# Raw token rows carried through the expert slots and scattered back, with the third normalisation moved from ScalarE to GpSimd

## The reference

```
x = x + cross_attention_16_heads(layernorm(x), ctx)     # each head sees 4 rows of ctx
x = x + moe(layernorm(x))                               # top 1 of 16 experts
x = x + causal_attention(layernorm(x), ctx, ctx)        # one head, 77 rows of ctx
x = x + dense_ffn(layernorm(x)) + peer_experts(layernorm(x))

moe(h): gate = softmax(h @ Wg); idx = argmax(gate)
        loc = number of earlier tokens that chose the same expert
        row idx*256 + loc of a table holds the token, if loc < 256 (else its output is 0)
        y = relu(row @ w1[idx]) @ w2[idx];  output = y * gate[idx]
```

## Time and profile before

| what | value |
|---|---|
| median of three runs | 505.94 us (505.74 to 507.4) |
| profiled execution, span from first to last instruction | 506.4 us |
| PE, DVE, ACT, POOL busy over the span | 83%, 72%, 68%, 66% |
| mean granted TensorE clock | 0.892 of full |
| stage A, until the first product with w1 | 0 to 121.86 us |
| stage B, until the last matmul | 121.86 to 184.4 us |
| gathers before the first transpose of stage C | 184.4 to 195.1 us |
| stage C, until the first product search of stage D on DVE | 195.1 to 254.6 us |
| stage D | 254.6 to 506.4 us |

### The profile page before, as it was taken

The page is one execution under the profiler, slowest core; times in us unless marked ns, Lnnn a source line. Parts: engine busy times, 40 slices in busy tenths (PEclk is TensorE's granted clock), DMA queues, the critical chain, the costliest instruction groups (busy, mean ns, idle before and its releaser), DMA issues.

```text
span 506.4 us, 9519 instructions
## 1 busy us (share of the span) xinstructions
PE 420.5 (83%) x2592; PEld 342.9 (68%) x2592; DVE 363.5 (72%) x1469; ACT 345.3 (68%) x652; POOL 334.1 (66%) x269
## 2 busy tenths in 40 slices
PE   4877887964999953986877999999999999999877
PEld 3766766733998852875645776767767767777667
DVE  3457885520222214789689999999999999999991
ACT  1462546241222222699779999999999999999995
POOL 5235877762000017564049999999999999999995
PEclk9795998575999995568598999999999999999998
DMA  6982000102567611111000000000000000000000
GB/s 202 344 225 83 27 21 22 43 26 67 143 198 214 191 38 53 36 53 32 1 12 10 14 20 10 21 21 21 21 10 16 16 21 21 21 13 19 10 12 21
DMA packets 42417, 29.70 MB, mean 59 GB/s; under 512 B 4155, under 2 KB 38555, under 8 KB 42395
## 3 DMA queue, kind: packets, MB, share of 16 engines
q1 hardware_dynamic: 38539, 22.85, 15.7%
q0 software_dynamic: 2624, 6.30, 3.6%
q10 hardware_dynamic: 1232, 0.31, 0.3%
HBM read 18.95 MB, written 8.39 MB: 54 GB/s over the span
## 4 chain that ended last, share of the span: by engine, by line
POOL 31%; issue 9%; DVE 5%; ACT 5%; PE 3%; POOLq 1%; ACTq 0%; DVEq 0%
POOL arena_sb L497 20%; POOL arena_sb L489 10%; DVE picked_sb L1486 4%; ACT arena_sb L745 1%; ACT xh_sb L531 1%; ACT arena_sb L737 1%; ACT sc_sb L667 1%; PE banks L1062 1%; PE banks L1070 0%; PE banks L1016 0%; PE banks L1105 0%; PE banks L1114 0%; PE banks L1164 0%; PE banks L1034 0%; DVE cbn_sb L1368 0%
## 5 line engine op out<-in xcount | busy, mean ns | idle before, releaser
L497 POOL TENSOR_TENSOR arena_sb<-arena_sb,picked_sb 128x1096 f32<-128x1096 f32 (+1 forms) x46 | 152.2, 3337 | 10.6 <-DVE picked_sb L1486 8.1
L1486 DVE SCALAR_TENSOR_TENSOR picked_sb<-arena_sb,best_sb,banks 128x548 f32<-128x548 f32 x128 | 90.3, 778 | 0.2 <-POOL arena_sb L489 0.2
L745 ACT ACTIVATE arena_sb<-arena_sb,bsum_sb 128x548 f32<-128x548 f32 x124 | 83.1, 743 | 7.5 <-DVE bsum_sb L1494 5.4
L461 POOL DMA_INDIRECT picked_sb<-made,made_row_sb x32 | 30.9, 966 | 79.2 <-DMA made<-arena_sb 70.3
L489 POOL TENSOR_TENSOR arena_sb<-near_sb,sim_y_sb 128x1024 f32<-128x1024 f32 (+1 forms) x32 | 74.2, 2344 | 2.4 <-DVE near_sb L1451 2.3
L1105 PEld LDWEIGHTS banks<-ident_sb,arena_sb 128*128 128x128 f32 x496 | 57.6, 153 | 24.3 <-issue 16.6
L737 ACT ACTIVATE arena_sb<-arena_sb 128x2192 f32<-128x2192 f32 x32 | 65.6, 2049 | 0.2
L1105 PE MATMUL banks<-ident_sb,arena_sb 128*128 128x128 f32 x496 | 61.5, 278 | 4.5 <-ACT h_sb L723 3.1
L1095 PE MATMUL banks<-w_down_t_sb,h_sb 128*128 128x128 f32 x256 | 36.5, 289 | 9.3 <-DVE x_all_sb L1505 9.0
L1070 PEld LDWEIGHTS banks<-xt_sb,w_up_t_sb 128*128 128x128 f32 x256 | 31.1, 191 | 18.1 <-ACT w_t_sb L527 16.7
L1114 PE MATMUL banks<-up_e_sb,w_t_sb 128*128 128x128 f32 x256 | 36.0, 286 | 5.5 <-DVE picked_sb L1486 4.4
(11 more groups left out here) (182 smaller groups left out, 895.0 us busy)
## 6 DMA issues: line engine op xcount, KB each, us to landing
w_sb<-w SPq DMA_DIRECT2D x32, 256.0 KB, 3.2
x_all_sb<-x SPq DMA_DIRECT2D x8, 256.0 KB, 3.2
slots<-arena_sb POOLq DMA_DIRECT2D x4, 512.0 KB, 8.9
arena_sb<-slots SPq DMA_DIRECT2D x16, 128.0 KB, 3.1
made<-arena_sb SPq DMA_DIRECT2D x16, 128.0 KB, 1.9
xt_sb<-x_t_sb SPq DMA_DIRECT2D x32, 64.0 KB, 1.8
out<-x_all_sb SPq DMA_DIRECT2D x32, 64.0 KB, 1.5
ctx_t_sb<-ctx_t SPq DMA_DIRECT2D x8, 154.0 KB, 3.8
```

The lines of the kernel that those rows point to most:

```text
L497: pool.tensor_tensor(pp[p][:, heads, :], pp[p][:, heads, :], picked[p][:, heads, :], ALU.mult).then_inc(weighed, 1)
L745: ins = act.activation(pp[p][:, h, :], pp[p][:, h, :], ACT.Silu, scale=bsum[p][:, h:h + 1])
L1486: ins = dve.scalar_tensor_tensor(out=picked[p][:, h, :], in0=vv[p][:, h, 0:WIDE], scalar=best[p][:, h, TOP - 1:TOP], in1=scores_of(p), op0 ...
```

## The change

The tile of x in SBUF gets four more columns per token: `rstd`, shift, gate and the token's number. These 132 columns go to the slots as they are, so x is scattered raw.

- Stage A: `slot_rows` (ACT) goes. `choice_exps(j)` and `gates(j)` move forward in their lists, because `scatters(j)` now waits for the gate. `rows` has one instruction fewer. SP stores the eight blocks of x to a DRAM table `tokens`, each when its attention is added.
- Stage B: ACT normalises the loaded rows first (`slots_centred`, two activations per expert); PE's transposes wait for that. `rows_out` becomes two instructions that multiply by the gate and add the raw row. The store to `made` goes. POOL copies the token numbers of the loaded rows and issues two indirect transfers per expert that scatter the finished rows into `tokens`. SP loads the next rows of a buffer only after `rows_out` of the old ones and the copy of their numbers.
- Stage C: `gathers` and `combine` go. SP waits for all scatters and loads x back in eight transfers. `biases3` and ACT's `last_tokens` go; POOL normalises with four instructions per group.

```
@@ gpsimd
+            step(pool.iota(token_row, [[P, NT], [0, 1]], 0, 1))
...
             def scatters(i, p):
-                pool.wait_ge(xh_ready, 2 * i + p + 1)
+                pool.wait_ge(gate_ready, i + 1)
...
+            for e in range(NE):
+                b, nth = e % NBUF, e // NBUF
+                if nth:
+                    pool.wait_ge(y_out[b % 2], 32 * (2 * nth - 1 + b // 2))
+                pool.wait_ge(xe_in[b], 32 + 16 * nth)
+                pool.tensor_copy(token_of[b][:, :], xe[b][:, :, AT_TOKEN].bitcast(U32)).then_inc(token_of_ready, 1)
+                pool.wait_ge(tokens_kept, 16 * NB)
+                pool.wait_ge(y_ready, 1 + e + 1)
+                hold(pool, token_of_ready, 1 + e + 1)
+                for n in two:
+                    pool.indirect_dma_start(out=tokens, out_offset=bass.IndirectOffsetOnAxis(
+                        ap=token_of[b][:, n:n + 1], axis=0), in_=ye[b % 2][:, n, :], in_offset=None).then_inc(y_out[b % 2], 16)
+
+            def last_tokens(g):
                 p = g % 2
                 pool.wait_ge(croot3_ready, g + 1)
                 if g >= 2:
+                    pool.wait_ge(xt3_mm, g - 1)
+                for t in range(BT):
+                    ins = pool.tensor_scalar(xh[p][:, t, :], x_all[:, g * BT + t, 0:D], cmv3[p][:, t, 0:1], crstd[p][:, t:t + 1],
+                                             ALU.subtract, ALU.mult)
+                ins.then_inc(cxh_ready, 1)
@@ scalar, stage B
+                def slots_centred(b):
+                    act.wait_ge(xe_in[b], 32 + 16 * i)
+                    act.wait_ge(xet_mm, 1 + NBUF * i + max(b - 1, 0))
+                    for n in two:
+                        ins = act.activation(xe_n[b % 2][:, n, :], xe[b][:, n, 0:D], ACT.Identity,
+                                             bias=xe[b][:, n, AT_SHIFT:AT_SHIFT + 1], scale=xe[b][:, n, AT_RSTD:AT_RSTD + 1])
+                    ins.then_inc(xen_ready, 1)
+                slots_centred(0)
+                slots_centred(1)
                 slots_out(0)
                 slots_out(1)
                 for b in range(NBUF):
+                    if b + 2 < NBUF:
+                        slots_centred(b + 2)
                     relu_lo(b)
@@ sync
+            for half in range(NB):
+                sp.wait_ge(x1_ready, half + 1)
+                sp.dma_start(token_rows(half), x_all[:, half * BT:half * BT + BT, 0:D]).then_inc(tokens_kept, 16)
...
+                    sp.wait_ge(token_of_ready, 1 + NBUF * i + b + 1)
+                    sp.wait_ge(y_ready, 1 + NBUF * i + b + 1)
+                    load_slots(i + 1, b)
+                    load_expert(sp, i * NBUF + NBUF + b, b)
+            for p in two:
+                sp.wait_ge(y_out[p], 32 * (NE // 2))
+            for g in range(NB):
+                sp.dma_start(x_all[:, g * BT:g * BT + BT, 0:D], token_rows(g)).then_inc(x2_in[g], 16)
@@ vector
+            def rows_out(e):
+                b = e % NBUF
+                dve.wait_ge(y_mm, 1 + e + 1)
+                if e >= 2:
+                    dve.wait_ge(y_out[e % 2], 32 * (e // 2))
+                for n in two:
+                    ins = dve.scalar_tensor_tensor(out=ye[e % 2][:, n, :], in0=bank[6 + e % 2][:, n * D:(n + 1) * D],
+                                                   scalar=xe[b][:, n, AT_GATE:AT_GATE + 1], in1=xe[b][:, n, 0:D],
+                                                   op0=ALU.mult, op1=ALU.add)
+                ins.then_inc(y_ready, 1)
```

More of the change, by code:

```diff
@@ L171, in program @@
         w2 = [sb(f"w2_{b}", [P, FC, D]) for b in range(NBUF)]
-        made_row = sb("made_row", [P, NT], U32)
-        yg = [sb(f"yg{p}", [P, BT, D]) for p in two]
-        rows_of = [xh, yg]
+        token_of = [sb(f"token_of{b}", [P, 2], U32) for b in range(NBUF)]
         sc = [sb(f"sc{p}", [P, BT, TK]) for p in two]
@@ L263, in program, with token_rows @@
         out_rows = a["out"].rearrange("b t d -> t b d")
+        def token_rows(half):
+            return tokens[half * BT * P:(half + 1) * BT * P, :].rearrange("(b t) d -> t b d", b=BT)
         def begin(eng, sems, by=1):
@@ L326, in _ @@
             with sp.Fori(0, NE // NBUF - 1) as i:
-                experts(i, True)
-            experts(NE // NBUF - 1, False)
+                for b in range(NBUF):
+                    sp.wait_ge(token_of_ready, 1 + NBUF * i + b + 1)
[6 more added lines that the diff above has]
+                sp.dma_start(x_all[:, g * BT:g * BT + BT, 0:D], token_rows(g)).then_inc(x2_in[g], 16)
             def load_d(i):
@@ L530, in normalise @@
                 for t in range(BT):
-                    ins = act.activation(dst[:, t, :], x_all[:, first + t, :], ACT.Identity,
+                    ins = act.activation(dst[:, t, :], x_all[:, first + t, 0:D], ACT.Identity,
                                          bias=bias[:, t:t + 1], scale=scale[:, t:t + 1])
@@ L1288, in turn @@
                 values(i, 0)
+                if j is not None:
+                    gates(j)
                 shift(i, 1)
@@ L1355, in tile, with relu_hi @@
-            def tile(n):
-                return x_all[:, n, :]
-            def combine(g):
-                dve.wait_ge(gathered[g], 16 * BT)
-                for n in range(g * BT, g * BT + BT):
-                    ins = dve.scalar_tensor_tensor(out=tile(n), in0=made_x[:, n, :], scalar=gate[:, n:n + 1],
-                                                   in1=tile(n), op0=ALU.mult, op1=ALU.add)
-                ins.then_inc(x2_ready, 1)
+            def relu_hi(e):
+                if e >= 2:
+                    dve.wait_ge(y_mm, 1 + e - 1)
+                dve.wait_ge(h_mm, 1 + e + 1)
+                dve.tensor_scalar(he[e % 2][:, 2:4, :], bank[3 + 2 * (e % 2)][:, :].rearrange("p (c s) -> p c s", c=2),
+                                  0.0, None, ALU.max).then_inc(h_hi, 1)
@@ L1365, in statistics @@
+            relu_hi(0)
+            relu_hi(1)
+            for e in range(2, NE):
+                rows_out(e - 2)
+                relu_hi(e)
+            rows_out(NE - 2)
+            rows_out(NE - 1)
+            def tile(n):
+                return x_all[:, n, 0:D]
             def statistics(g, bn, mv, done):
@@ L1415, in _ @@
             step.turn()
-            combine(0)
             statistics2(0)
@@ L1419, in _ @@
             biases(0)
-            combine(1)
             statistics2(1)
@@ L1425, in _ @@
             for g in range(2, NB):
-                combine(g)
                 add_attention(g - 2)
```

175 lines of the change are left out of this document (56 added, 119 removed).

## The result

The changed kernel takes 513.65 us (median of four runs, 512.8 to 517.4); the kernel before, run beside it, takes 506.2. The ratio is 1.0165, with a 95% interval of 1.0125 to 1.0206. The same kernel run again later gave 513.1 and 1.0176 (1.0107 to 1.0245). I had forecast 501.8, so not only the size but the sign is wrong.

The account below looks back on a forecast made before the run. Limits taken: a chain through all engines in stage A, PE in B, PE or DVE and ACT by clock in C. Terms -0.5+1.0+0-1.2-3.4+0 = -4.1 from 506.4 give 502.3, less 0.46: 501.8 us, range 497.0 to 507.0.

Parts of the forecast that it names:

- The latency of this link stays the same: Stage C, POOL's normalisation: 2.2 us per group replaces POOL's small operations plus ACT's 1.65; cost 0, from -2 to +4.
- rival 3: Slower: in stage C POOL's normalisation becomes the wait replacing the combine; 510.8 us at 1.0 per instruction; chance 0.14.
- Stage C, turns: Turns without combine and ACT's normalisation: 5.3 us at full clock, 6.46 otherwise; -3.4 us, from -6.1 to +0.2.
- rival 2: Clock stays at half in stage C, PE limits turns at 6.46, only the start gains: 505.4 us; chance 0.20.
- Rival 1: Clock stays up in stage C, turns at 5.3 throughout, -6.1 instead of -3.4: 499.1 us; chance 0.18.
- First expert: Stage B, start: ACT normalises the loaded rows before PE, so the first product with w1 comes 1.0 us later.
- Stage C, start: PE's first transpose after scatters and loads, without a combine, at 193.9 instead of 195.13: -1.2 us, from -2.0 to 0.
- Stage B, steady: PE stays the limit at 3.86 us per expert, the added work is covered: cost 0, range 0 to +3.
- Stage A, -0.5: Stage A: ACT's activations removed against scatters waiting for the gate; -0.5 us, from -1.5 to +1.0.

Follow-up runs that it names:

- pool_wide: Changed kernel with POOL normalising the third tokens in two 128x512 instructions instead of four 128x128 ones: 506.3 us, ratio 1.0007.
- a_dummy: Changed kernel with ACT's 32 activations of stage A put back as work whose result nobody reads: 516.2 us, ratio 1.0191.
- n_act: Changed kernel with the third normalisation back on ACT, POOL keeping only the two small bias operations: 506.5 us, ratio 0.9997.
- n_dve_end: Changed kernel with the third normalisation on DVE, behind shares, and the last group's roots3 ahead of the similarities: 506.8 us, ratio 1.0009.
- pool_wide_end: Changed kernel with POOL normalising in two 128x512 instructions and the last group's roots3 ahead of the similarities: 505.6 us, ratio 0.9979.

## Why the prediction was wrong

**The step that failed first** is "The latency of this link stays the same ... cost nothing", with 0.55 us for POOL's instruction, from `centre`. The form takes 0.794. My bound of 1.1 held it, and rival 3 named the point from which it decides, 0.75. So the price was inside what I had worked out. The rate was not: rival 3 counted 5 us for each us that the four instructions grow ("one transpose in two turns, 0.5 us a turn"). The link is passed once in every turn, and twice at the end. From the link of the wide form (2.16) to the narrow (3.12), 0.96 us, the time goes from 506.3 to 513.65: 7.6 us for each us. One passage for each of the eight groups would make 8. Rival 3 at the measured price would have given 501.8 + 5 x 0.98 = 506.7.

**The second step that failed** is "Stage C, turns", -3.4. I divided the turn by engines (DVE 5.3, ACT 4.7, PE 6.46 or less) and let the largest win. That leaves out the chain through all four, which is not the load of any engine: POOL's idle time before each normalisation, 4.20 us, released by ACT, was the sign of it, and in the rows of before the same wait of PE for `xh_sb` stands in the earlier trace rows. With the short link on POOL the forecast turns do appear (5.2 to 5.5 at a clock of 0.78 to 1.00, 6.43 at 0.50), in two turns of seven, and the time is then 506.3, near the 505.4 of rival 2, where most turns run at half clock. Of the 3.4, the combine is worth about 1.4 in all, part of which is the start of the stage. Rival 1's clock did not come with fewer waits either: in two turns of pool_wide running (210.60 to 223.46) PE is busy 6.41 of 6.43 us and has 0.50 in both.

**What was right.** First expert +1.0: measured 1.3 (5.73 to 5.86 in four executions with the old code, 6.99 to 7.25 in thirteen with the new). Stage C, start, -1.2: measured 1.3 to 1.4 (10.7 to 10.9 against 9.3 to 9.5). Stage B, steady, 0: 62.5 to 63.2 us before, 62.5 to 63.8 after, and at the loop's first end POOL's copy of numbers (134.27) is not even late: `rows_out` of the same expert ends at 134.77, and PE waits 0.35 us before its next products. For the last expert of the loop the copy, 137.79, is again the earlier one: its `rows_out` now stands behind `relu_hi` of the next expert and ends at 139.98. Stage A, -0.5, is not settled: the last scatter starts at 112.2, 112.4, 115.8 and 116.0 in the four old executions and between 111.7 and 114.4 in twelve new ones. By a_dummy's median the eight activations a turn would be worth 2.5 to 3, where I had counted 0.8 for the part that I saw; against it stands the gate's wait. The turn of the earlier trace rows on POOL and DVE now:

```profile
84.55 0.19 POOL L435 CAST scatter_row_sb<-row_f_sb 128x8 uint32<-128x8 f32 x1
84.96 0.21 DVE L1277 RECIPROCAL x_all_sb<-lsum_sb 128x8 f32<-128x8 f32 x1
86.05 1.11 POOL L441 DMA_INDIRECT slot_rows<-x_all_sb,scatter_row_sb  x1 [1.31 <-DVE x_all_sb L1277]
```

From the end of the rows (84.74) to the gate (85.17) are 0.43 us, where I had 0.25.

**The sum again** with what was measured: first expert and start cancel, the combine gives about 1.4, stage A at most one or two; n_act, which is all of this, came out at 0.9997 of the kernel before, where these terms would allow up to 3 us less. That difference I cannot place. The link adds 7.1 (506.5 to 513.65). Of the two rivals to this account, PE at half clock is excluded by the turn of 6.98 at 0.76, and by n_act, where the turns fell; POOL's work as such by pool_wide.

Smaller mistakes: I took a timed run to be 0.46 us under the span. It is about 1.9 above it (512.76 for the span of 510.8), so the profiled execution of before would be one of 508.3, 2.1 above the median of 506.2, and that of the changed kernel was 0.9 under its median; that is why the two spans differ by 4.4 and the medians by 7.5. The terms of stage C's turns add up to -3.3 and not -3.4, and in rival 3 the 0.46 was taken off twice: its 9.0 less 4.1 gives 510.8 against the median. None of this changes the outcome.

The Trainium skill's warning, GPSIMD Engine Reference, 4.1 Engine selection, was right in its advice, VectorE for elementwise work: DVE's four took 1.12 us, POOL's 3.12 (n_dve_end and pool_wide_end, 506.8 and 505.6, are not told apart by their intervals, so POOL's wide form did as well). Its reason fits less well: near line rate for one input, about half for two. On POOL the one-input form over 128x512 took 1.92 us and the two-input form 1.27; here the measurement decides.

## What to carry to other kernels

Before you price a move between engines, follow one turn of the loop round by its waits until you are back at the same instruction; if the sum of that round is the turn, an operation in it counts in full in every turn, and one outside it counts for little, however busy its engine is (the combine, 1.05 us of DVE in each turn, was worth about 1.4 in all). Price the very form of the instruction (operands, operations, width): four narrow ones and two wide ones of the same engine differed by 1 us a passage, which here was the whole loss. When two profiles of one kernel spread by 4 us, compare stages by intervals between events of one execution, and let timed runs decide the rest.

## What the runs showed of the hardware

A POOL elementwise instruction on fp32 got longer with operands and operations: 128x128 with one constant 0.528 us, with two per-partition scalars and two operations 0.791; and a tensor-tensor over 128x512 with a broadcast second input, 1.042, cost less than one with two full inputs, 1.268, and less than a tensor-scalar with two constants, 1.922.

DVE's `biases`, a 128x4 operation with both inputs in SBUF, took 0.49 us instead of 0.16 when it met POOL's second wide instruction: it started at 222.89 and ended at 223.38, with POOL's 1.04 from 222.32 ending at 223.36. The Trainium skill, SBUF — State Buffer, section "SBUF: two separate sides", describes a port pair that DVE, with two SBUF inputs, and GpSimd, when it reads SBUF, take in turn for a whole instruction; the two ends, 0.02 us apart, agree with it. POOL's narrow instruction in the changed kernel does not: `biases` began and ended inside one, in 0.25 us, so there the wait for the whole instruction did not come, and the measurement decides.

```profile
216.24 0.79 POOL L484 TENSOR_SCALAR xh_sb<-x_all_sb,cmv_sb,crstd_sb 128x128 f32<-128x128 f32 x1
216.45 0.25 DVE L1394 TENSOR_TENSOR cbias_sb<-cmax_sb,cscale_sb 128x4 f32<-128x4 f32 x1
```
